# First attention's probabilities times values in three passes of split halves, and the shared expert's first input split moved into that expert's program

## The reference, cut to what matters

```python
probs = softmax(einsum('blhd,bmhd->bhlm', q, k_full) * scale + mask)     # 16 heads of 128, 4 value heads
out = einsum('bhlm,bmhd->blhd', probs, v_full)
out = out.reshape(B, L, 2048) @ wo                                       # keys: 64 of the context + up to 512
...
shared = silu(x @ sw_gate) * (x @ sw_up) @ sw_down                       # 512 -> 704 -> 512
```

## Time and profile before

| what | value |
|---|---|
| median of 3 runs | 1999.44 us (1999.3 to 1999.74) |
| profiled execution | 1994.72 us, span 1992.9 us |
| TensorE busy | 1852.5 us, 93% |
| TensorE weight load busy | 1323.4 us, 66% |
| VectorE busy | 1099.0 us, 55% |
| ScalarE busy | 1038.4 us, 52% |
| GpSimd busy | 962.9 us, 48% |

### The profile page before, as it was taken

How to read it: one execution, slowest core, us unless ns; L and a number is a source line. 1 busy time by engine, 2 the same in 40 slices (tenths; PEclk the granted TensorE clock), 3 DMA queues, 4 the chain that set the end, 5 groups by cost and what they waited for, 6 DMA issues and landing times. The chain is left out here.

```text
span 1992.9 us, 27633 instructions
## 1 busy us (share of the span) xinstructions
PE 1852.5 (93%) x9796; PEld 1323.4 (66%) x9796; DVE 1099.0 (55%) x2264; ACT 1038.4 (52%) x2251; POOL 962.9 (48%) x865
## 2 busy tenths in 40 slices
PE   6999999999999999999998999989999778859998
PEld 4666766766766666666765877769999656624443
DVE  4544544446455654556444648424343678748886
ACT  3555656554554545544544321126666367647775
POOL 4544565444653445544531100028888355537774
PEclk8999999999999999999999999989999989979999
DMA  7111111111012111111011100147889750000000
GB/s 235 45 50 50 48 34 47 62 31 50 34 33 71 48 52 47 34 49 39 25 47 67 65 22 22 43 144 203 233 226 273 184 134 1 1 0 23 21 18 27
DMA packets 112952, 141.18 MB, mean 71 GB/s; under 512 B 37408, under 2 KB 68128, under 8 KB 112624
## 3 DMA queue, kind: packets, MB, share of 16 engines
q1 hardware_dynamic: 105648, 122.63, 19.6%
q0 software_dynamic: 7168, 16.78, 4.0%
HBM read 104.78 MB, written 29.36 MB: 67 GB/s over the span
## 5 line engine op out<-in xcount | busy, mean ns | idle before, releaser
L743 POOL TENSOR_TENSOR a_xcl<-xT,a_xch 128x512 fp32r<-128x512 f32 x64 | 82.4, 1287 | 322.9 <-ACT a_xch L558 322.9
L898 PE MATMUL a_A<-a_pT,a_vf 128*128 128x512 f32 (+1 forms) x448 | 236.7, 610 | 0.9 <-ACT a_pT L574 0.9
L848 PE MATMUL a_S<-a_kT,a_qT 128*128 128x288 f32 (+3 forms) x640 | 209.7, 426 | 4.8 <-ACT a_qT L586 3.1
L659 DVE TENSOR_REDUCE a_nmax<-a_S 128x1 f32<-128x192 f32 (+3 forms) x256 | 138.1, 551 | 83.2 <-PE a_S L849 81.9
L564 ACT ACTIVATE a_pr_odd<-a_S,a_nmax 128x320 f32<-128x320 f32 (+1 forms) x128 | 80.9, 633 | 156.1 <-DVE a_nmax L659 154.8
L120 PE MATMUL a_A<-a_wlo,a_xch 128*128 128x512 f32 x256 | 153.7, 600 | 6.3 <-DVE a_qT L655 6.3
L848 PEld LDWEIGHTS a_S<-a_kT,a_qT 128*128 128x128 f32 x640 | 114.8, 189 | 53.8 <-issue 26.8
L574 ACT ACTIVATE a_pT<-a_TR 128x512 f32<-128x512 f32 (+1 forms) x224 | 132.3, 591 | 33.0 <-PE a_TR L888 32.2
L2404 PE MATMUL f_HH<-w12T,f_f_xqT 128*128 128x512 bf16 x512 | 125.0, 394 | 14.8 <-DVE f_h L2261 13.0
L564 ACT ACTIVATE a_pr_even<-a_S,a_nmax 128x192 f32<-128x192 f32 (+1 forms) x128 | 67.0, 525 | 135.1 <-DVE a_nmax L659 135.0
L1503 POOL TENSOR_TENSOR e_wlo<-expert_raw,e_whi 128x1408 fp32r<-128x1408 f32 x32 | 102.8, 3232 | 68.0 <-ACT e_whi L1673 68.0
(11 more groups left out here) (389 smaller groups left out, 5193.3 us busy)
## 6 DMA issues: line engine op xcount, KB each, us to landing
a_pw<-in_L_ffn_w_dram SPq DMA_DIRECT2D x96, 256.0 KB, 2.8
expert_raw<-in_L_ffn_w_gate_dram SPq DMA_DIRECT2D x16, 704.0 KB, 7.9
expert_raw<-in_L_ffn_w_up_dram SPq DMA_DIRECT2D x16, 704.0 KB, 9.8
expert_raw<-in_L_ffn_w_down_dram SPq DMA_DIRECT2D x16, 512.0 KB, 10.2
tern<-a_tern SPq DMA_DIRECT2D x48, 128.0 KB, 1.9
x_res<-in_x_dram SPq DMA_DIRECT2D x4, 1024.0 KB, 9.3
a_raw<-in_L_xattn_wq_dram SPq DMA_DIRECT2D x4, 1024.0 KB, 6.5
a_raw<-in_L_xattn_wo_dram SPq DMA_DIRECT2D x4, 1024.0 KB, 5.5
```

The lines of the kernel that those rows point to most:

```text
L659: ve.tensor_reduce(nmax[:, s % 2, i:i + 1], pair(s, i), AX.X, ALU.max, negate=True).then_inc(s_max, 1)
L743: pool.tensor_tensor(xcl[:, t % 2], xT[:, :, tok(t)], xch[:, t % 2].bitcast(F32), ALU.subtract).then_inc(xlo_ready, 1)
L848: pe.matmul(bank[:, lo:hi], qT[:, t % 2, hq], kT[:, par(t), lo:hi], start=True, stop=hi < nk)
L898: last = pe.matmul(A[:, A_USE["V", t, 0][0]], vf[r, par(t), i], pT[r, i % 2], start=i == 0, stop=i == nkt - 1)
```

## The change

Turned probabilities and values are kept as two fp32r halves. ScalarE's copy writes the high half (`pTh`); a new VectorE step `l`i subtracts it from the PSUM bank to give the low half (`pTl`), and only that frees the bank and admits `V`i, which becomes three passes. VectorE's `v` gets one more instruction (`vfl`). Context values land in `vcs` and are split by a new step `a` on both engines, once per batch. `L` is gone; `split_x(0)` runs at the start of the shared expert's program, ahead of the weight splits.

```diff
-    DVE_SLOT = "M0 M1 N0 L D X v M2 N1 N2 j0 j1 M3 N3 B E A"
+    DVE_ORDER = {-3: "A0 A1 X0 A2 X1 A3 X2 X3 b u c0 t c1", -2: "v E A", -1: "v X E A", 
+                 "first": "M0 M1 N0 D X v M2 N1 N2 M3 N3 a B E A",
+                 0: "M0 M1 N0 D l0 X v M2 N1 l1 N2 l2 j0 j1 M3 l3 N3 l4 B E A",
+                 1: "M0 M1 N0 D l0 X v M2 N1 N2 l1 j0 j1 M3 N3 B E A",
+                 2: "M0 M1 N0 D l0 X v M2 N1 N2 l1 a j0 j1 M3 l2 N3 B E A",
+                 3: "M0 M1 N0 D l0 X v M2 N1 l1 N2 l2 j0 j1 M3 l3 N3 B E A"}
...
-        vf = s_.sb("vf", [P, 2, BT + 1, HD])
+        vfh, vfl = (s_.sb(f"vf{q}", [P, 2, BT + 1, HD], F32R) for q in "hl")
+        vcs = s_.sb("vcs", [P, HD])
...
-        pT = s_.sb("pT", [P, 2, GH * P])
+        pTh, pTl = (s_.sb(f"pT{q}", [P, 2, GH * P], F32R) for q in "hl")
...
-                    if name == "L" and s == SLOTS:
...
+                    if name == "l" and live(s, -1):
+                        t = s - 1
+                        until(ve, pT_ready, turn(i), t, m)
+                        ve.tensor_tensor(pTl[0:rows(i), i % 2], TR[0:rows(i), TR_USE["P", t, i][0]], pTh[0:rows(i), i % 2].bitcast(F32),
+                                         ALU.subtract).then_inc(p_lo, 1)
+                    if name == "a" and context(s) is not None:
+                        n = context(s)
+                        ve.wait_ge(vh_ready, n + 1)
+                        ve.tensor_tensor(vfl[0:T, n % 2, 0], vcs[0:T], vfh[0:T, n % 2, 0].bitcast(F32), ALU.subtract).then_inc(vl_ready, 1)
...
+                        ve.tensor_tensor(vfl[:, par(t), 1 + t % BT], bank[:, HD:2 * HD], vfh[:, par(t), 1 + t % BT].bitcast(F32), ALU.subtract)
...
-                        sem, count = {"P": (pT_ready, turn(before[2])), "T": (qT_ready, tile), "K": (kT_ready, tile),
+                        sem, count = {"P": (p_lo, turn(before[2])), "T": (qT_ready, tile), "K": (kT_ready, tile),
...
-                        until(pe, pT_ready, turn(i), t, m)
+                        until(pe, p_lo, turn(i), t, m)
-                        last = pe.matmul(A[:, A_USE["V", t, 0][0]], vf[r, par(t), i], pT[r, i % 2], start=i == 0, stop=i == nkt - 1)
+                        last = mm3(pe, A[:, A_USE["V", t, 0][0]], vfh[r, par(t), i], vfl[r, par(t), i], pTh[r, i % 2], pTl[r, i % 2],
+                                   i == 0, i == nkt - 1)
...
+                split_x(0)
                 for j, hi in enumerate((gh, uh)):
...
+                split_x(0)
                 for j in range(2):
                     for k in range(KD):
                         split_weight(j, k)
```

More of the change, by code:

```diff
@@ L122, in mm3, with attention0_stage @@
     return pe.matmul(out, lhs_hi, rhs_hi, start=False, stop=last)
-def attention0_stage(nc, x, ident, tri, gates, xT, xh, xl, next_weights, next_loaded, xn_dram, x_in, ctx_in, wq_in, wk_in, wv_in, wo_in, wkc_in, wvc_in, qw_in, kw_in, g_xattn, g_ffn,
+def attention0_stage(nc, x, ident, tri, gates, xT, next_weights, next_loaded, xn_dram, x_in, ctx_in, wq_in, wk_in, wv_in, wo_in, wkc_in, wvc_in, qw_in, kw_in, g_xattn, g_ffn,
                      consts, kctx_dram, vctx_dram, ffn_in, tern_dram, total_dram, mean):
@@ L146, in attention0_stage @@
                  -1: "x v d0 k t r f y",
[2 rows of a table removed]
[2 rows of a table added]
                  1: "x e0 j0 e1 g0 j1 v u e2 r g1 n w j2 e3 k t o f",
[1 row of a table removed]
[1 row of a table added]
                  3: "x e0 j0 e1 g0 j1 v e2 r g1 n g2 j2 e3 g3 k t o f"}
-    DVE_SLOT = "M0 M1 N0 L D X v M2 N1 N2 j0 j1 M3 N3 B E A"
-    DVE_ORDER = {-3: "A0 A1 X0 A2 X1 A3 X2 X3 b u c0 t c1", -2: "v E A", -1: "v X E A", "first": DVE_SLOT,
-                 0: DVE_SLOT, 1: DVE_SLOT, 2: DVE_SLOT, 3: DVE_SLOT}
+    DVE_ORDER = {-3: "A0 A1 X0 A2 X1 A3 X2 X3 b u c0 t c1", -2: "v E A", -1: "v X E A",
[5 rows of a table added]
     POOL_ORDER = {-3: "r0 r1 r2 r3 x w c0", -2: "x c1 r", -1: "q x r", "first": "x q p0 p1 r",
@@ L186, in row, with context @@
         return n if BT <= n < PERIOD else n - AGAIN if PERIOD <= n - AGAIN < PERIOD + BT else None
+    def context(s):
+        return 0 if s == 0 else batch_next(s) // BT if s % BT == 2 and live(batch_next(s), 0) else None
     def bank_order(firsts):
@@ L311, in attention0_stage @@
         wkc = odd[:, 0:KD * D].rearrange("p (k n) -> p k n", k=KD)
-        wvc = (pT[:, 0], pT[:, 1], vf[:, 1, 0:KVH].rearrange("p j d -> p (j d)"), kT[:, 1, 0:D])
+        wvc = [xT[:, k, B * L // 2:B * L // 2 + D] for k in range(KD)]
         kc = qT[:].rearrange("p t (h d) -> p t h d", h=KVH)
@@ L344, in attention0_stage @@
         xn_stored = [s_.sem(f"xn_stored{u}") for u in range(2)]
-        xh_ready, xl_ready = s_.sem("xh_ready"), s_.sem("xl_ready")
+        p_lo, vh_ready, vl_ready = s_.sem("p_lo"), s_.sem("vh_ready"), s_.sem("vl_ready")
         piece_loaded = [s_.sem(f"piece_loaded{u}") for u in range(2)]
@@ L401, in load_values @@
                     rows_of = slice(n % B * T, (n % B + 1) * T)
-                    sp.dma_start(vf[0:T, n % 2, 0], vctx_dram[rows_of, n // B * HD:(n // B + 1) * HD]).then_inc(cv_loaded, 16)
+                    if n > 0:
+                        sp.wait_ge(vl_ready, n)
+                    sp.dma_start(vcs[0:T], vctx_dram[rows_of, n // B * HD:(n // B + 1) * HD]).then_inc(cv_loaded, 16)
                 def store_keys(c):
@@ L536, in do @@
                         act.activation(gates[:], graw[:].rearrange("p l s -> p (l s)"), ACT.Tanh).then_inc(gates_ready, 1)
-                    if name == "L" and s == SLOTS:
-                        act.wait_ge(xT_ready, PERIOD + BT)
-                        for k in (0, 2):
-                            act.activation(xh[:, k:k + 2], xT[:, k:k + 2, 0:L], ACT.Copy).then_inc(xh_ready, 1)
                     if name == "w" and (s == BEGIN or s % PERIOD in (1, PERIOD - 2)):
@@ L570, in do @@
                                        scale=rec[:, s % 2, h:h + 1]).then_inc(p_act, 1)
+                    if name == "a" and context(s) is not None:
+                        n = context(s)
+                        act.wait_ge(cv_loaded, 16 * (n + 1))
+                        if n >= 2:
+                            act.wait_ge(o_full, tile(BT * (n - 1) - 1))
+                        act.activation(vfh[0:T, n % 2, 0], vcs[0:T], ACT.Copy).then_inc(vh_ready, 1)
                     if name == "g" and live(s, -1):
@@ L573, in do @@
                         until(act, p_turned, turn(i), t, m)
-                        act.activation(pT[0:rows(i), i % 2], TR[0:rows(i), TR_USE["P", t, i][0]], ACT.Copy).then_inc(pT_ready, 1)
+                        act.activation(pTh[0:rows(i), i % 2], TR[0:rows(i), TR_USE["P", t, i][0]], ACT.Copy).then_inc(pT_ready, 1)
                     if name == "o" and live(s, -1):
@@ L592, in do @@
                         act.activation(sq[:, GH], bank[:, 0:HD], ACT.Square)
-                        act.activation(vf[:, par(t), 1 + t % BT], bank[:, HD:2 * HD], ACT.Copy).then_inc(kv_act, 1)
+                        act.activation(vfh[:, par(t), 1 + t % BT], bank[:, HD:2 * HD], ACT.Copy).then_inc(kv_act, 1)
                     if name == "f" and live(s, 2):
@@ L629, in do @@
                         ve.tensor_scalar(xn[:, u], x[:, t % PERIOD], mv[:, u, 0:1], rstd[:, u:u + 1], ALU.subtract, ALU.mult).then_inc(xn_ready, 1)
[L630 to L633, removed]
                     if name == "b":
@@ L894, in do @@
                             if t % BT == 0:
-                                until(pe, cv_loaded, lambda v: 16 * batch(v), t, m)
-                        until(pe, pT_ready, turn(i), t, m)
+                                until(pe, vl_ready, batch, t, m)
+                        until(pe, p_lo, turn(i), t, m)
                         r, nkt = slice(0, rows(i)), t % BT + 2
-                        last = pe.matmul(A[:, A_USE["V", t, 0][0]], vf[r, par(t), i], pT[r, i % 2], start=i == 0, stop=i == nkt - 1)
+                        last = mm3(pe, A[:, A_USE["V", t, 0][0]], vfh[r, par(t), i], vfl[r, par(t), i], pTh[r, i % 2], pTl[r, i % 2],
+                                   i == 0, i == nkt - 1)
                         if i == nkt - 1:
@@ L1066, in gate_up @@
                     n = NI * b + t
-                    if t == 0 and b > 0:
-                        pe.wait_ge(x_lo, b)
+                    if t == 0:
+                        pe.wait_ge(x_lo, b + 1)
                     if n >= 2:
@@ L1150, in split_x @@
                 def split_x(b):
-                    act.wait_ge(gu_full, NI * b)
+                    if b > 0:
+                        act.wait_ge(gu_full, NI * b)
                     act.activation(xh[:], xT[:, :, b * L:(b + 1) * L], ACT.Copy).then_inc(x_hi, 1)
+                split_x(0)
                 for j, hi in enumerate((gh, uh)):
@@ L1223, in split_x @@
                 def split_x(b):
-                    ve.wait_ge(x_hi, b)
+                    ve.wait_ge(x_hi, b + 1)
```

(4 more changed lines are left out.)

## The result

The changed kernel took 2122.86 us, median of 4 runs (2120.2 to 2132.2); the kernel before 1999.59 (1999.3 to 1999.99). The ratio is 1.0623, 95% interval 1.0595 to 1.0651: 6% slower. The forecast was 2110, the range 2020 to 2140. The profiled execution of the changed kernel is the longest of the four, with a span of 2130.4 us and a granted clock of 0.954; the shortest had 0.963. The spans of the two profiles are 137.5 us apart and the medians 123.3: the one profile is a long execution of its kernel, the other (1994.72 us) a short one.

A forecast was written before the change was run, and what follows sets the result against it. PE, busy 93%, was taken as the bound. The profiled 1994.7 + 14 (non-ternary slots) + 64.5 (ternary) + 29 (clock) + 3.3 (expert's start) + 0.5 (attention's end) = 2106; the median 4.7 above gave 2110 us, range 2020 to 2140.

The forecast's parts named there:

- the walk: Attention slots followed step by step: l delays later steps; slot 31 ends 0.8 us later, T at 556.02 instead of 555.03.
- C: Rival, attention: PE stays the bound and the waits are taken up, so the kernel gets faster, 1975 us; chance 0.13.
- D: Rival, the three passes: weight loads don't overlap or a pass costs more than 0.24 us; 2155 us; chance 0.05.
- B: Rival, attention: only the ordinary waits, j0 and j1 still hide under the scores in ternary slots; 2022 us; chance 0.12.
- The ternary term: Attention's ternary slots: j0 and j1 start after l2 and delay M3 and T; +64.5 us, bounds -14 and +90.
- The clock: 18 long PE gaps in ternary slots each drop the clock, at 1.6 us: +29 us, bounds 0 and 48.
- Rival A: The stalls in the attention are real but the clock stays up: 2081 us; chance 0.22.
- The other slots: The 40 attention slots that aren't ternary, 10 rounds of +1.4 us: +14 us, bounds -24 and about +45.
- The start of the shared expert: First pass there waits for the moved split: +3.3 us, bounds 0 and +5; the attention's end adds +0.5.
- The gain: On PE in the attention, three passes save 0.17 us in each of 224 multiplications: 38 us less work.

The follow-up runs named there:

- e4: The changed kernel with VectorE's order alone changed: j0 moved into a gap, j1 behind N3; 2051.98 us, ratio 1.0283.
- e6: The changed kernel with ScalarE's order alone changed: copies ahead of the exponentials they stood behind, j2 at the slot's end; 2029.33 us, ratio 1.0162.
- e7: The changed kernel with one swap on VectorE, N2 ahead of l1 in kinds 0 and 3; 2108.31 us, ratio 1.055.
- e5: The changed kernel, all work kept, with new orders on both ScalarE and VectorE, X still behind l0; 1994.01 us, ratio 0.9984.
- e11: The changed kernel with new orders on ScalarE and VectorE, and X ahead of l0; 1968.9 us, ratio 0.9862 to the kernel before.
- e1: The changed kernel without step l, the low half set to zero once, all three passes running; 1999.75 us, ratio 1.0023.
- e9: The changed kernel without step l, and with step a moved to the end of kind 2 on both engines; 1981.32 us, ratio 0.9919.
- e3: The kernel before with only the split of the first 512 rows moved into the shared expert's program; 2002.46 us, ratio 1.0038.
- e2: The changed kernel with all its waits, but each multiplication one float32 matmul, low halves made and unused; 2146.59 us, ratio 1.0772.
- e8: The kernel before, one float32 matmul and no step l, with such new orders on ScalarE and VectorE; 1979.63 us, ratio 0.9912.

## Why the prediction was right

**The mechanism.** It held step by step: in slot 31 every step stands within 0.2 us of the walk, and T at 7.61 against 7.63 us behind V0; in slot 39 M3 stands right behind j1 and T 10.08 behind V0 against 10.39; e4, e6 and e7 came out within 11, 1 and 1 us of what was expected of them. That the cause is order and not work is shown by e4, e5 and e11, which hold all the work of the change, its other buffers and DMA waits too. Of the rivals, C (faster, the waits are taken up) fell with the result; its half microsecond at V1 was really missing (the 0.31 named at V1, and a start 0.48 after it was due). D (dear passes) fell with e1, where a slot of kind 0 is 0.81 shorter. B (only the ordinary waits) fell with M3 behind j1 in slot 39 and with the 81.7 us of the ternary slots.

**The sum.** The number is closer than its parts, and part of that is luck. The forecast's terms add up to 111 us on the profiled execution, and the two profiles are 137.5 apart: 26 short. Of the medians 111 and 123 are to be compared, 13 short, because the execution profiled of the changed kernel was a long one and that of the kernel before a short one.

**The ternary term**, 64.5 + 29 with the clock, measured 81.7 in the profile. Without a slow clock, kind 0 is +3.38 (3.5 foretold), kind 1 +1.21 (1.5), kind 2 +2.1 (2.2). Kind 3, with a fall of the clock in each of the six, is +5.3 (3.56 + 1.6). (The upper bound of this term is +97 where it is worked out as half as long again, not +90; nothing rests on it.)

**The clock** was over-counted. I had 18 falls at 1.6 us. In the profile of the changed kernel the granted clock fell in 10 of these 18 slots, the six of kind 3 and four of the six of kind 2, and in two slots of kind 1 that I had not counted (one of them had a fall before the change too). Kind 0 has its gap as well, 2.90 us ahead of T in slot 36, but the passes behind it are 0.23 apart. From V0 to V0, slot 36 and slot 39 (PEclk is the third number from the end):

```profile
691.40:711.88 20.48, 16.98 (x89) 12.63 (x88) 12.29 (x29) 8.08 (x21) 7.13 (x9) 1.00 0.14 42
745.96:766.61 20.65, 16.80 (x85) 13.20 (x84) 11.38 (x24) 8.34 (x20) 6.25 (x6) 0.92 0.13 38
```

The four slots of kind 2 with a fall are 3.7 longer than before and the two without 2.1, which gives the price of a fall once more: 1.6. Twelve falls less one at that price are 18 us, an estimate, where 29 were foretold. Rival A, no fall, was wrong too.

**The other slots**, 14 foretold, measured 42.5. This is the term that was mis-sized. Kinds 0, 1 and 3 were right to about 0.2 us in the steady state (+0.81, -0.07, +0.82 against +0.6, -0.2, +0.8); kind 2 is +0.66 by its medians against +0.25. Two steps were priced at nothing and weren't. The large one is X. It stands behind l0, and PE's waits for it, up to slot 9 and from slot 60 on, went from 3.9 to 18.7 us; 14 of these 15 us lie in the slots of this term, half of the 28.5 that are missing, and 1 ahead of the first V0. With X ahead of l0 they went back (e11). The small one is `a`. In slot 30 of the changed kernel PE's last scores for M3, VectorE's `a` and M3 are:

```profile
578.60 0.22 PE L868 MATMUL a_S<-a_causal,a_ident_b 128*128 128x128 bf16 x1
578.74 0.56 DVE L713 TENSOR_TENSOR a_vfl<-a_vcs,a_vfh 64x128 fp32r<-64x128 f32 x1
579.23 0.61 DVE L668 TENSOR_REDUCE a_nmax<-a_S 128x1 f32<-128x448 f32 x1
```

The scores are done at 578.82 and M3 starts 0.4 us later, as `a` ends; T stands 5.79 behind V0 there, and the walk had 537.75 - 532.44 = 5.31. Over ten ordinary slots that is 4 us. The 18 us of e9 are the price of `a` in a kernel without `l` and not in this one. The other 10 us or so are not taken apart. The sum slots gained 23.6 us, some 10 of them waits for X, and ScalarE's j steps, which stand in the same chain, were not in my walk, but no run separates what they cost. The two errors, clock and ordinary slots, had opposite signs, so the total is closer than its parts.

**The start of the shared expert**: 3.3 + 0.5 foretold, 5.1 measured, 2.9 of them the split itself (e3). From the last V0 to the last tile's projection it is 8.15 us where it was 7.53, the 0.5 foretold. The projection itself takes 1.6 us longer, because most of its passes run 0.43 apart, at 1.2 GHz; that fall was not foreseen.

**The gain** of 0.17 per multiplication is real where nothing else waits: kind 0 and kind 1 in e1. In no kernel did all 38 us come through: 24 between e2 and the changed one, 11 between e8 and e11.

## What to carry to other kernels

In this kernel a new step on an engine that is half idle cost its place in that engine's order, not its length: write down what stood behind it, and who on other engines waits for that, for each step, the smallest too. Where a reader of a buffer is added, the buffer's next user waits for it as well; here T waited 85 us and V 10. When a change adds work in a hand-written order, re-walk the order before judging the work: the same instructions took 2123 us in one order and 1969 in another, and the old kernel had 18 us of its own in it.

## What was not expected of the hardware

Gaps of the same length were sometimes followed by passes at 1.2 GHz and sometimes not. In the changed kernel T of the ternary slots of kind 2 waits 3.45 to 3.48 us each time, and the clock fell in four of six. After the 2.90 us of kind 0 it fell in none of six; in e2, with 2.71 to 2.73 us at the same place, it fell in five of six. After 1.53 and 1.55 us it fell once and not once. One fall cost 1.6 us in most of the places where it can be read from slots of equal content, and 1.2 us in ternary slots of kind 0 in e7 (21.05 against 19.89). What decides was not tried.
